# A graph network's edge sort on one core: payload in one product, ranks folded by sevens, run ends on another engine

## The reference, cut to what matters

```python
edge_w = (att_s[:, row] + att_n[:, col]) * adj_vals
msgs = edge_w[..., None] * feat_nei[:, col, :]
agg = jax.vmap(lambda m: jax.ops.segment_sum(m, row, num_segments=N))(msgs)
```

## Time and profile before

| | |
|---|---|
| median of 3 runs | 5031.49 us (5025.98 to 5047.4) |
| the profiled execution | 5030.4 us, span 5028.8 us |
| busy, share of the span | PE 73%, PEld 56%, DVE 73%, ACT 50%, POOL 72% |
| sort, first round to last (L1293 on) | about 137 to 764 us |
| first gather of the edge loop (L668) | 808.09 us |

### The profile page before, as it was taken

How to read it: one execution, slowest core, us unless ns; L and a number is a source line. 1 busy time by engine, 2 the same in 40 slices (tenths; PEclk the granted TensorE clock), 3 DMA queues, 4 the chain that set the end, 5 groups by cost and what they waited for, 6 DMA issues and landing times.

```text
span 5028.8 us, 67492 instructions
## 1 busy us (share of the span) xinstructions
PE 3674.9 (73%) x17277; PEld 2816.9 (56%) x17277; DVE 3651.0 (73%) x8530; ACT 2489.6 (50%) x5972; POOL 3615.5 (72%) x4003
## 2 busy tenths in 40 slices
PE   0787764667767676666767678888888888888886
PEld 0676553455545555555555456666666666666664
DVE  4899994666666666666666557777777777777776
ACT  0454224444444444444444356666666666666664
POOL 1567886777777777777777567777777777777774
PEclk9999996888898888989888889999999999999997
DMA  3231003445455555444554556565555665666555
GB/s 103 78 91 53 7 7 93 141 148 148 149 148 153 149 148 150 148 148 148 148 153 146 108 156 172 172 177 176 173 174 174 177 175 172 176 177 175 172 172 114
DMA packets 393065, 710.59 MB, mean 141 GB/s; under 512 B 77542, under 2 KB 233410, under 8 KB 392654
## 3 DMA queue, kind: packets, MB, share of 16 engines
q0 software_dynamic: 161104, 434.80, 31.0%
q1 hardware_dynamic: 231582, 271.44, 17.7%
HBM read 622.28 MB, written 85.27 MB: 141 GB/s over the span
## 4 chain that ended last, share of the span: by engine, by line
POOL 57%; issue 19%; PE 4%; DMA 3%; DVE 1%; ACT 1%; DVEq 0%; ACTq 0%; POOLq 0%
POOL arena L668 30%; POOL arena L680 26%; DMA arena<-d_p,tabS 2%; PE ps L1069 1%; PE ps L1098 1%; DMA arena<-d_t,tabD 1%; PE ps L1047 0%; DVE arena L1547 0%; PE ps L1035 0%; DVE big L1537 0%; PE ps L1080 0%; ACT tabE L900 0%; ACT arena L815 0%; POOL arena L660 0%; ACT tabE L887 0%
## 5 line engine op out<-in xcount | busy, mean ns | idle before, releaser
L680 POOL DMA_INDIRECT arena<-d_p,tabS x1628 | 1571.0, 965 | 548.5 <-issue 488.1
L668 POOL DMA_INDIRECT arena<-d_t,tabD x1628 | 1554.9, 955 | 509.4 <-issue 493.8
L1047 PE MATMUL ps<-arena 128*128 128x256 f32 x3256 | 999.9, 461 | 639.2 <-ACT arena L815 523.0
L815 ACT ACTIVATE arena<-arena,tabE 128x256 f32<-128x256 f32 x1628 | 693.4, 496 | 1034.2 <-DMA arena<-d_t,tabD 1034.0
L1047 PEld LDWEIGHTS ps<-arena 128*128 128x128 f32 x3256 | 706.3, 227 | 863.7 <-DVE big L1402 565.4
L1069 PE MATMUL ps<-arena 128*128 128x256 f32 x3256 | 870.4, 397 | 180.9 <-DVE big L1537 171.1
L1080 PE MATMUL ps<-big,tabE 128*128 x3256 | 809.1, 387 | 93.9 <-DVE arena L1547 82.5
L1537 DVE SCALAR_TENSOR_TENSOR big<-big,tabK,ps 128x256 f32 x1628 | 774.5, 476 | 93.7 <-DVE big L1537 83.1
L1402 DVE TENSOR_TENSOR big<-big,ps 128x256 f32 x1628 | 681.4, 419 | 200.9 <-DVE big L1402 191.4
L1069 PEld LDWEIGHTS ps<-arena 128*128 128x128 f32 x3256 | 595.2, 194 | 407.2 <-DVE big L1537 227.1
L915 ACT ACTIVATE arena<-arena 128x1024 f32<-128x1024 f32 x407 | 430.2, 1057 | 740.3 <-DVE arena L1547 740.1
(11 more groups left out here) (249 smaller groups left out, 4073.4 us busy)
## 6 DMA issues: line engine op xcount, KB each, us to landing
arena<-d_loc SPq DMA_DIRECT2D x407, 256.0 KB, 4.0
arena<-d_t,tabD POOLq DMA_INDIRECT x1628, 2.8
arena<-d_p,tabS POOLq DMA_INDIRECT x1628, 3.4
arena<-in_xT_dram SPq DMA_DIRECT2D x96, 256.0 KB, 3.6
d_t<-arena SPq DMA_DIRECT2D x49, 256.0 KB, 2.1
d_xp<-arena SPq DMA_DIRECT2D x49, 256.0 KB, 2.6
arena<-d_xp SPq DMA_DIRECT2D x49, 256.0 KB, 4.0
d_x<-arena SPq DMA_DIRECT2D x49, 256.0 KB, 2.6
```

Source lines behind the costliest of these rows:

```text
L668: e.indirect_dma_start(out=GB[g][:, k, :], out_offset=None, in_=d_t, in_offset=bass.IndirectOffsetOnAxis(ap=tabD[:, j, k:k + 1], axis=0)). ...
L680: e.indirect_dma_start(out=G1[j % 8][:, k, :], out_offset=None, in_=d_p, in_offset=bass.IndirectOffsetOnAxis(ap=tabS[:, j, k:k + 1], axis= ...
L815: a = e.activation(GB[q][:, k, :], GB[q][:, k, :], ACT.Copy, scale=tabE[:, j - 1, 1, k:k + 1])
L1047: m = e.matmul(PS[4 + 2 * q + k // 2][:, (k % 2) * 256:(k % 2) * 256 + 256], OH[q][:, k, :], GB[(g - 1) % 4][:, k, :], start=True, stop=True)
```

## The change

- `payp` is laid out (edge, part, twice), and the five products become one of 16 x 5 x 48 = 3840 elements per lane.
- The rank sums are kept 7 wide in place of 15: 14 matmuls of 16 x 7 = 112 columns for `PR`, two of 112 and one of 16 for `EQ`. The fold reads 224 elements in place of 480.
- `run` and `cm` go. ScalarE writes the run ends of every batch side by side (`ends`, 101 values) and the offset, in three small activations, one before and two after the eviction `EV`. The scatter waits for `s_of`. After the sort VectorE subtracts neighbours (98 x 100) and takes the maximum.
- VectorE's order is fold, `OHS`, attention product, `OHR`, `PR`, attention sum, payload, leak. ScalarE's eight scalings stand ahead of its attention eviction.

The diff, cut to its core; the blocks that only move are told above, and the other parts of `payp` change their layout as part 1 does.

```diff
-        payp = b16(take(8000)).rearrange("p (a c t) -> p a c t", a=5, t=2)
+        payp = b16(take(8000)).rearrange("p (c a t) -> p c a t", a=5, t=2)
...
@@ gpsimd, sort
                     e.tensor_tensor(tk, ev[:, 0:2 * CAP], ev[:, 2 * CAP:4 * CAP], ALU.add).then_inc(S("s_k0"), 1)
-                    e.tensor_scalar(offi[(g - 3) % 4][0:NT, :], run[0:NT, :], lim[0:NT, :], None, ALU.min).then_inc(S("s_k1"), 1)
-                    e.tensor_scalar(cm[0:NT, :], cm[0:NT, :], ev[:, 5 * CAP:5 * CAP + 1], None, ALU.max).then_inc(S("s_k1"), 1)
-                    waitn(e, "s_k1", (j - 3) * 3 + 1)
-                    e.tensor_tensor(run[0:NT, :], run[0:NT, :], ev[:, 5 * CAP:5 * CAP + 1], ALU.add).then_inc(S("s_k1"), 1)
...
-                    waitn(e, "s_k1", (j - 2) * 3)
+                    waitn(e, "s_of", j - 2)
@@ scalar, sort
...
                 q = j - 2
                 if 0 <= q < NP:
...
+                if a:
...
+                if not done(j, NB, 2):
+                    waitn(e, "s_run", q)
+                    waitn(e, "s_of", q)
+                    e.activation(over[0:NT, :], ends[0:NT, q:q + 1], ACT.Relu, scale=-1.0, bias=lim[0:NT, :]).then_inc(S("s_ov"), 1)
+                    waitn(e, "s_k0", q - 1)
+                    waitn(e, "s_k2", (q - 1) * 2)
+                    waitn(e, "s_O", q + 1)
+                    e.activation(EV[h][0:NT, :], PS[4 + h][0:NT, 0:5 * CAP + 1], ACT.Copy).then_inc(S("s_ev"), 1)
+                    waitn(e, "s_ov", q + 1)
+                    waitn(e, "s_sc", 16 * (q - 3))
+                    e.activation(offi[q % 4][0:NT, :], over[0:NT, :], ACT.Identity, scale=-1.0, bias=lim[0:NT, :]).then_inc(S("s_of"), 1)
+                    waitn(e, "s_ev", q + 1)
+                    e.activation(ends[0:NT, q + 1:q + 2], EV[h][0:NT, 5 * CAP:5 * CAP + 1], ACT.Identity,
+                                 bias=ends[0:NT, q:q + 1]).then_inc(S("s_run"), 1)
@@ tensor, sort
-                    o = PS[2 + q][:, 0:15 * COLS]
-                    e.matmul(o, idb[0:LANES, :], EQ[q][0:LANES], start=True, stop=False)
-                    for k in range(6):
-                        e.matmul(o, idb[0:LANES, :], PR[q][0:LANES, :, 15 * k:15 * k + 15], start=False, stop=False)
-                    e.matmul(grid(o, 15)[:, :, 0:NT - 90], idb[0:LANES, :], PR[q][0:LANES, :, 90:NT], start=False, stop=True)\
-                     .then_inc(S("s_F"), 1)
+                    o = grid(PS[2 + q][:, 0:7 * COLS], 7)
+                    e.matmul(o, idb[0:LANES, :], EQ[q][0:LANES, :, 0:7], start=True, stop=False)
+                    e.matmul(o, idb[0:LANES, :], EQ[q][0:LANES, :, 7:14], start=False, stop=False)
+                    e.matmul(o[:, :, 0:1], idb[0:LANES, :], EQ[q][0:LANES, :, 14:15], start=False, stop=False)
+                    for k in range(NT // 7):
+                        m = e.matmul(o, idb[0:LANES, :], PR[q][0:LANES, :, 7 * k:7 * k + 7], start=False, stop=(k == NT // 7 - 1))
+                    m.then_inc(S("s_F"), 1)
@@ vector, preparation
-            P1(e.tensor_copy(payp[L, 1], doubled(wB[L])))
-            P1(e.tensor_tensor(junk[L], wB[L], payp[L, 1, :, 0], ALU.subtract))
+            P1(e.tensor_copy(payp[L, :, 1], doubled(wB[L])))
+            P1(e.tensor_tensor(junk[L], wB[L], payp[L, :, 1, 0], ALU.subtract))
@@ vector, sort
-                        e.tensor_reduce(RK[L], grid(PS[2 + h][L, 0:15 * COLS], 15).unsqueeze(2).to_broadcast([LANES, COLS, 2, 15]),
+                        e.tensor_reduce(RK[L], grid(PS[2 + h][L, 0:7 * COLS], 7).unsqueeze(2).to_broadcast([LANES, COLS, 2, 7]),
...
-                    for k in range(5):
-                        p = e.tensor_tensor(twos(PAY[h][L, :, k * CAP:(k + 1) * CAP]), twos(OHR[L]),
-                                            payp[L, k, bass.ds((j - 2) * COLS, COLS), :].unsqueeze(2).to_broadcast(b24), ALU.mult)
-                    p.then_inc(S("s_pay"), 1)
+                    b5 = [LANES, COLS, 5, CAP // 2, 2]
+                    e.tensor_tensor(PAY[h][L, :, 0:5 * CAP].rearrange("p c (a n t) -> p c a n t", a=5, t=2),
+                                    twos(OHR[L]).unsqueeze(2).to_broadcast(b5),
+                                    payp[L, bass.ds((j - 2) * COLS, COLS)].unsqueeze(3).to_broadcast(b5), ALU.mult).then_inc(S("s_pay"), 1)
@@ vector, tables
-            e.wait_ge(S("s_k1"), 3 * NB)
+            e.wait_ge(S("s_run"), NB)
+            run = ends[:, NB:NB + 1]
+            T1(e.tensor_tensor(made[B], ends[B, 1:NB + 1], ends[B, 0:NB], ALU.subtract))
+            T1(e.tensor_reduce(cm[B], made[B], AX.X, ALU.max))
```

More of the change, by code:

```diff
@@ L46 @@
 A_LOC = A_CHUNK + 10
-S_PREP = 10 + 13 + 6
-T_CNT = 7
+S_PREP = 9 + 13 + 6
+T_CNT = 9
 T_TILE = T_CNT + 3 + 14 + 5
@@ L321, in gnn @@
         dbase = take(100)
-        run, lim, tl, cm, ncnt, nrow, ovA, ovE, ovF = (take(1) for _ in range(9))
+        lim, tl, cm, ncnt, nrow, ovA, ovE, ovF, over = (take(1) for _ in range(9))
         offi = [take(1).bitcast(i32) for _ in range(4)]
@@ L328, in gnn @@
         cIe, tIe = (take(NC).bitcast(i32) for _ in range(2))
-        top = 128 + 100 * 19 + 8 + 9 + 6 + NC * 10
+        ends = take(NB + 1)
+        made = take(NB)
+        top = 128 + 100 * 19 + 8 + 9 + 6 + NC * 10 + 2 * NB + 1
         take = carve(A, top)
@@ L774, in sort @@
                     e.activation(EQ[h][0:LANES], EQ[h][0:LANES], ACT.Relu, scale=-1.0, bias=1.0).then_inc(S("s_eq"), 1)
[L775 to L783, removed]
                 q = j - 2
@@ L792, in sort @@
                     v.then_inc(S("a_gm"), 1)
+                if a:
+                    waitn(e, f"a_ts{g}", 16 * uses(i, g, 4, 4))
+                    waitn(e, "a_mm", j + 1)
+                    e.activation(TS[g % 4][:, :, 0:128], q2(PS[6 + h][:, 0:256]), ACT.Relu).then_inc(S("a_re"), 1)
+                if not done(j, NB, 2):
[12 more added lines that the diff above has]
+                                 bias=ends[0:NT, q:q + 1]).then_inc(S("s_run"), 1)
             sorting(e, sort)
             e.wait_ge(S("s_sc"), 16 * NB)
+            e.wait_ge(S("s_run"), NB)
             e.wait_ge(S("lc"), 16)
@@ L1185, in _ @@
             P1(e.tensor_scalar(tl, c[:, C_PID:C_PID + 1], float(LC), None, ALU.mult))
-            P1(e.tensor_copy(run, tl))
+            P1(e.tensor_copy(ends[:, 0:1], tl))
             P1(e.tensor_scalar(lim, tl, float(LC - CAP), None, ALU.add))
-            P1(e.memset(cm, 0.0))
             e.wait_ge(S("s_in"), 64)
@@ L1289, in sort @@
                 h = g % 2
+                q = j - 1
+                f = TS[q % 4][:, :, 0:128]
+                if not done(j, NB, 2):
+                    waitn(e, "s_or", j - 2)
+                    waitn(e, "s_F", j - 1)
+                    with nc.allow_low_precision("counts below 256"):
+                        e.tensor_reduce(RK[L], grid(PS[2 + h][L, 0:7 * COLS], 7).unsqueeze(2).to_broadcast([LANES, COLS, 2, 7]),
+                                        AX.X, ALU.add)\
+                         .then_inc(S("s_rk"), 1)
                 if not done(j, NB):
@@ L1294, in sort @@
                                     tfp[L, bass.ds(j * COLS, COLS), :].unsqueeze(2).to_broadcast(b49), ALU.is_equal).then_inc(S("s_oh"), 1)
-                if not done(j, NB, 1):
-                    waitn(e, "s_F", j - 2)
-                    waitn(e, "s_lb", j)
-                    e.tensor_tensor(PR[1 - h][L], ohs(OHS[(g - 1) % 4][L]),
-                                    LB[1 - h][L, :].unsqueeze(1).to_broadcast([LANES, COLS, NT]), ALU.mult).then_inc(S("s_pr"), 1)
-                q = j - 1
                 if 0 <= q < NP:
-                    f = TS[q % 4][:, :, 0:128]
                     waitn(e, "a_ar", q)
@@ L1306, in sort @@
                 if not done(j, NB, 2):
-                    waitn(e, "s_or", j - 2)
-                    waitn(e, "s_F", j - 1)
-                    with nc.allow_low_precision("counts below 256"):
-                        e.tensor_reduce(RK[L], grid(PS[2 + h][L, 0:15 * COLS], 15).unsqueeze(2).to_broadcast([LANES, COLS, 2, 15]),
-                                        AX.X, ALU.add)\
-                         .then_inc(S("s_rk"), 1)
                     waitn(e, "s_pay", j - 2)
@@ L1318, in sort @@
                      .then_inc(S("s_or"), 1)
+                if not done(j, NB, 1):
+                    waitn(e, "s_F", j - 2)
+                    waitn(e, "s_lb", j)
+                    e.tensor_tensor(PR[1 - h][L], ohs(OHS[(g - 1) % 4][L]),
+                                    LB[1 - h][L, :].unsqueeze(1).to_broadcast([LANES, COLS, NT]), ALU.mult).then_inc(S("s_pr"), 1)
                 if 0 <= q < NP:
```

11 lines of the change are left out of this document (6 added, 5 removed).

## The result

The kernel after takes 4969.56 us, median of 4 runs (4963.66 to 4971.06), against 5032.27 us for the kernel before (4 runs): a ratio of 0.9866, 95% interval 0.9849 to 0.9882. The profiled execution took 4970.86 us, span 4969.3, against 5030.4 before: 59.5 us less. The forecast was 95 us less.

The account below looks back on a forecast made before the run. VectorE was taken to bound the sort in both stretches. From 5030.4 us: -39 (48 rounds with attention), -57.5 (50 without), -2 drain, +4 preparation, -0.5 end of sort, giving 4935; range 4912 to 4988.

Parts of the forecast that it names:

- port share: VectorE's sort rounds: time lost to GpSimd halves with its operations, leaving 0.09 us with attention, 0.23 without; bounds nothing or all.
- preparation: Before the sort: five payload writes and two subtractions at 20-byte spacing cost +4 us, between nothing and +13.
- TensorE as the bound: Rival, sort: 17 matmuls at 0.11 us make TensorE's round 6.2, nothing saved with attention, 4972 us; chance 0.09.
- What bounds the kernel: Sort, about 150 to 764 us: VectorE bounds both stretches, 98% and 96% busy, never waiting for another engine.
- The merged product: VectorE's payload in the sort: one product of 3840 elements takes 2.07 us, 0.27 less than five apart.
- The expensive doubt, one element a cycle: Slower rival, payload product: 4.1 us start to start in place of 2.07, total 5134 us; chance 0.09.
- Fold and stalls: VectorE's sort rounds: fold of 224 elements takes 0.38 us, 0.30 start to start; interleaved order removes the 0.1 us stalls.
- GpSimd rival: Sort: GpSimd's three sums each enter only when a VectorE product ends, round about 6.0 us, total 5018; chance 0.05.
- ScalarE: Sort rounds: three run-end operations move there at about 0.17 us each, 0.5 us more a round, covered.
- End of the sort: VectorE's tables after the sort: start about 1 us earlier, two more small steps take 0.5 back, net -0.5 us.
- The first and the last rounds of the sort: Sort rounds outside the 48 with attention and 50 without: the drain rounds give -2 us.
- the clock: Part of the TensorE rival: more idle time or a lower granted clock (0.91 against 1.00) slows its matmuls; joint chance 0.09.

## Why the prediction was right, and where it was off

The time, 4969.56, lies in the range of 4912 to 4988, and the change made the kernel faster, as the forecast had it; but the forecast's 4935 was 35 us too low.

That the range held is in part luck. Its bounds for the port share were "nothing, or all", that is up to 0.18 and 0.47 us a round; the measured 0.48 and 0.60 lie above both. With all of that share (+15) and the worst preparation (+13 in place of +4) the high end would have been 4959. Only the allowance for TensorE as the bound, which did not come about, carried it past the measured time. By steps:

**What bounds the kernel** held: VectorE waits for no other engine in the rounds of either kernel (but once, 0.8 us for TensorE, between the two stretches after), and after its stalls on itself are gone too. (34 scatters in 200 us are 5.9 us a round and not "about 6.0"; the rounds are 5.999, so the value used was right.)

**The merged product** was priced right as a row (2.07; 2.06 measured). The expensive doubt, one element a cycle, is gone.

**Fold and stalls**: the fold takes 0.30 start to start, as said, and neither it nor `OHR` stalls.

**"Port share" is the step that failed.** "Half of the six operations go, so I keep half of what they cost": 0.09 and 0.23 us were kept; 0.48 and 0.60 were there. The step took the price as one of operations counted. But it is a price of meetings: three sums beside one product of 2.06 us cost more than six operations beside five products of 0.47. The merge is only a part of it: with five products, in the otherwise same kernel, the sums cost 0.34 and 0.35, already more than was kept, and the long product adds 0.14 and 0.25. With that the rounds are 0.34 and 0.36 longer than forecast. Measured from rounds before of 6.326 and 5.999 (the forecast used 6.30 and 6.0), 48 rounds gave 23.7 in place of 39, 50 gave 39.6 in place of 57.5: 33 of the missing 35 us. The forecast had read from the earlier trace rows what a product of VectorE does to GpSimd, and had even written down, for its GpSimd rival, that each sum gets in only when a product ends. It did not turn that round to VectorE's side. The Trainium skill (SBUF — State Buffer, "Who interferes with whom") says that a VectorE instruction with two SBUF inputs contends with a GpSimd one that reads SBUF; the sum that takes 1.99 us beside the payload product agrees. That the two exclude each other for the whole instruction, as the prediction puts that page's rule, does not explain VectorE's bill: the payload product at 299.48 had started before the sum at 300.10, and it took 2.28 us in place of 2.07.

**Preparation**: forecast +4. The five writes kept their 1.83 us, the two subtractions went to 3.00, +2.3 together; ahead of the sort 1.1 of it arrived (first `OHS` at 138.23 against 137.10). The loss is 1.17 us for 1600 elements that stand 20 bytes apart, 0.73 ns each. By the Trainium skill (Vector Engine (DVE) Microarchitecture Reference, measured stream behaviour) a stream that hops at every element loses some 0.65 cycle, which, with the 1.05 ns per element of the earlier trace rows as the cycle, would be 0.68 ns as an estimate: the two reads agree. The five writes put one pair every 20 bytes and lose nothing; the prediction's +7.6 from that page had counted them too, and there the measurement decides.

**ScalarE**: 0.28 us for a small activation (302.40 below), not 0.17; covered as forecast, since no VectorE instruction waits for it.

```profile
302.40 0.28 ACT L789 ACTIVATE arena<-arena 98x1 f32<-98x1 f32 x1
303.95 0.37 ACT L793 ACTIVATE big<-ps 98x241 f32<-98x241 f32 x1 [1.26 <-PE ps L1001]
304.22 0.29 ACT L796 ACTIVATE arena<-arena 98x1 int32<-98x1 f32 x1
```

**End of the sort**: VectorE's wait before its tables fell from 4.45 us to 2.87, and the two new steps take 0.76, so 0.8 us was gained (forecast 0.5). The first and the last rounds of the sort, forecast at -2, gave 0.3.

**The rest**: the tables start at 700.12 in place of 764.03 and the first gather at 744.92 in place of 808.09, 63.2 us earlier (forecast 95, at 713). The loops took back 3.7 of it: the last gather starts 59.5 us earlier. Why was not looked into.

**The rivals.** TensorE as the bound (4972) gives nearly the measured time and is still wrong: its 17 rank matmuls take 1.03 us start to start (305.20 to 306.23; forecast 0.88), and it is TensorE that waits for VectorE.

```profile
305.20 0.22 PE L985 MATMUL ps<-big 125*128 125x112 bf16 x1 [0.33 <-DVE big L1326]
...
305.35 1.04 PE L989 MATMUL ps<-big 125*128 125x112 bf16 x14
...
601.35 1.84 PE L1001 MATMUL ps<-big 125*128 125x241 bf16 x16 [0.94 <-DVE big L1335]
```

Nor did the clock turn against it: between 600 and 700 us the granted clock is 1.00, the 2.4 GHz level, in place of a mean of 0.91, and the placing matmuls take 1.84 us behind 0.94 us of idle time, where they took 3.38 behind 2.24. A time that fits a rival does not speak for it.

GpSimd as the bound (5018) was nearer to what happened than its chance of 0.05. GpSimd is full in both stretches, as it says, and its sums get in late. What it had otherwise is the bill: no engine waits for GpSimd in either stretch, and the time is lost in rows of VectorE that grow longer. With five products, when GpSimd has time left, a part of the price (0.34 and 0.35) stays; whether the rest comes from GpSimd being full or from the long product itself was not separated.

## What to carry to other kernels

Price a GpSimd operation beside a busy VectorE by what it meets, on both sides, not by its own length; and before merging short VectorE products into a long one, look at what slips in between them now. Merging was worth 0.27 us a round where GpSimd did no sums and 0.02 to 0.13 where it did. In this kernel the small sums of matmul results are cheaper on the bound engine, out of PSUM (0.33 us a round), than next to it (0.48 to 0.60), provided that they stand where their operands are ready.

## What the runs showed of the hardware that was not expected

- The scatter on GpSimd took between 0.97 and 2.9 us in the mean of a stretch, by the kernel, and lengthened no VectorE row where GpSimd did no sums.
- Sums without the scatter cost VectorE 0.10 and 0.18 us a round, sums with it 0.48 and 0.60, the scatter alone nothing: the prices don't add.
- A read of one bf16 value every 20 bytes made a 1600-element subtraction 3.00 us in place of 1.83; writes of pairs every 20 bytes cost nothing.
- GpSimd's first sum started 1.60 and 3.60 us after its operand was ready, round after round, while neither it nor VectorE waited for the other: two full engines kept step with no semaphore between them.
